# A recommendation tower in one kernel: first-layer weight first in the load queue, id tables over ScalarE's queue, context split and context transposes moved behind the weight tables

## The reference

```python
e = jnp.stack([tbl_0[ids[:, 0]], ..., tbl_25[ids[:, 25]]], axis=1)       # (512, 26, 32)
x1 = einsum('bik,bjk,hij->bhk', e, e, W1) + b1                           # (512, 128, 32)
x2 = einsum('bik,bjk,hij->bhk', x1, e, W2) + b2                          # (512, 128, 32)
z = concatenate([x1, x2], axis=1).sum(axis=-1)                           # (512, 256)
h = concatenate([z, dense_ctx], axis=1)                                  # (512, 272)
h = maximum(h @ W_top1 + b_top1, 0)                                      # 272 -> 512
h = maximum(h @ W_top2 + b_top2, 0)                                      # 512 -> 256
y = h @ W_top3                                                           # (512, 1)
```

## Time and profile before

| | |
|---|---|
| median of 3 runs | 152.55 us (152.45 to 153.67) |
| the profiled execution's own time | 151.98 us |
| its span, first to last instruction | 150.2 us |
| PE busy | 129.0 us (86%) |
| DVE busy | 103.0 us (69%) |
| POOL busy | 87.8 us (58%) |
| ACT busy | 73.9 us (49%) |
| mean granted TensorE clock | 0.966 of full speed |

### The profile page before, as it was taken

How to read it: one execution, slowest core, us unless ns; L and a number is a source line. 1 busy time by engine, 2 the same in 40 slices (tenths; PEclk the granted TensorE clock), 3 DMA queues, 4 the chain that set the end, 5 groups by cost and what they waited for, 6 DMA issues and landing times.

```text
span 150.2 us, 5238 instructions
## 1 busy us (share of the span) xinstructions
PE 129.0 (86%) x2218; PEld 114.3 (76%) x2218; DVE 103.0 (69%) x351; ACT 73.9 (49%) x201; POOL 87.8 (58%) x96
## 2 busy tenths in 40 slices
PE   5335999983988689988999998899999889699994
PEld 5323666753987579988879998887999877599992
DVE  7889583999999999789159969937994993000000
ACT  1220488487767874718658401363930146590042
POOL 3787777777788777777777777777777100000000
PEclk9955599999999999999999999999999999999999
DMA  6976438620013130100103220011332000311000
GB/s 116 387 157 176 117 135 213 194 74 20 13 18 59 40 82 13 18 13 13 18 18 61 72 54 13 14 18 18 60 83 48 5 0 4 52 45 54 0 0 1
DMA packets 9065, 9.36 MB, mean 62 GB/s; under 512 B 3089, under 2 KB 8047, under 8 KB 8862
## 3 DMA queue, kind: packets, MB, share of 16 engines
q1 hardware_dynamic: 5678, 7.55, 17.5%
q0 software_dynamic: 2816, 1.45, 7.1%
q10 hardware_dynamic: 548, 0.04, 0.3%
HBM read 7.99 MB, written 1.04 MB: 60 GB/s over the span
## 4 chain that ended last, share of the span: by engine, by line
PE 60%; DVE 17%; SPq 8%; DMA 7%; ACT 3%; issue 3%; DVEq 0%
PE h2y L746 16%; PE h2y L751 8%; DMA octet<-in_octet_ids 7%; PE ring L702 7%; PE ring L710 5%; DVE l L569 5%; PE h2y L801 5%; SPq L310 3%; SPq L314 3%; PE ring L730 3%; PE ring L680 2%; PE ring L739 2%; PE h1p L792 2%; DVE vh_in L443 2%; PE ring L703 2%
## 5 line engine op out<-in xcount | busy, mean ns | idle before, releaser
L350 POOL DMA_INDIRECT emb<-in_tbl,idx x88 | 86.9, 988 | 28.2 <-issue 26.5
L746 PE MATMUL h2y<-t_in,v_in 128*128 128x128 f32 x208 | 24.3, 276 | 0.0
L746 PEld LDWEIGHTS h2y<-t_in,v_in 128*128 128x128 f32 x208 | 23.7, 192 | 0.2
L667 PE MATMUL ring<-w1s,w2t 128*128 128x352 f32 x52 | 18.3, 515 | 3.5 <-DVE w1s L404 3.5
L912 ACT COPY t_in<-ring 128x416 f32<-128x416 f32 x32 | 15.2, 537 | 11.3 <-PE ring L703 11.3
L702 PEld LDWEIGHTS ring<-r,l 64*64 64x64 f32 x512 | 16.4, 134 | 4.5 <-issue 2.1
L702 PE MATMUL ring<-r,l 64*64 64x52 f32 x512 | 18.1, 220 | 1.6 <-issue 1.2
L667 PEld LDWEIGHTS ring<-w1s,w2t 128*128 128x128 f32 x52 | 11.1, 215 | 9.9 <-DVE w1s L404 3.6
L703 PE MATMUL ring<-r,l 64*64 64x52 f32 x512 | 18.3, 220 | 0.0
L703 PEld LDWEIGHTS ring<-r,l 64*64 64x64 f32 x512 | 16.5, 134 | 0.0
L569 DVE TENSOR_TENSOR l<-sg_b,l 128x192 f32<-128x192 f32 (+5 forms) x72 | 16.1, 299 | 0.2
(11 more groups left out here) (133 smaller groups left out, 209.5 us busy)
## 6 DMA issues: line engine op xcount, KB each, us to landing
w2t<-in_L_rec_W SPq DMA_DIRECT2D x1, 1664.0 KB, 7.0
emb<-in_tbl,idx POOLq DMA_INDIRECT x88, 3.0
wt<-in_W_top SPq DMA_DIRECT2D x2, 512.0 KB, 8.8
small_tbl<-in_tbl SPq DMA_DIRECT2D x8, 125.0 KB
octet<-in_octet_ids SPq DMA_DIRECT2D x1, 750.0 KB
gram_scratch<-t_in SPq DMA_DIRECT2D x4, 169.0 KB
gram<-gram_scratch SPq DMA_DIRECT2D x4, 126.0 KB
w<-in_L_rec_W SPq DMA_DIRECT2D x1, 338.0 KB, 7.3
```

The costliest lines, as they stand in the source:

```text
L350: pool.indirect_dma_start(out=emb[:, g, f * K:(f + 1) * K], out_offset=None, in_=a[f"tbl_{f}"][:, :], in_offset=bass.IndirectOffsetOnAxis( ...
L667: last = pe.matmul(ps[:, 0:PR + MIX], w2t[:, c, :], w1_of[c // NH], start=True, stop=True)
L746: last = pe.matmul(z2p, v_in[:, j, :], t_in[:, j, :], start=(start and j == j0), stop=(stop and j == j1 - 1))
```

## The change

Four things are moved; no instruction of the computation is added or removed.

1. On SP's queue W1 goes ahead of W2.
2. The two parts of `octet` and `place_in` are issued by ACT, behind its small rows, where SP issued them before.
3. DVE does the W1 tables (L384 to L409) right behind its first clears; the context split, the clear of `t_ac` and the clear of half of `R` come behind them. `one_hot_rest` goes ahead of `split_wt1c`.
4. On PE (and ACT) the "small" entry of `pre` is first, and the context transposes stand between mix 8 and mix 9. In the first group's `z_group` the second look-up for group 1 stands behind the first 13 products, where it stood behind the gram products.

```diff
-OH_FIRST, OH_FIRST_AT = 2, 18
+OH_FIRST, OH_FIRST_AT, CTX_AT = 2, 18, 9
...
-        pre = [("ctx", 0, 0), ("small", 0, 0)]
-        pre += [("mix", x, 1) for x in range(NF)]
+        pre = [("small", 0, 0)]
+        pre += [("mix", x, 1) for x in range(CTX_AT)] + [("ctx", 0, 0)] + [("mix", x, 1) for x in range(CTX_AT, NF)]
...
             sp.dma_start(idx[:, :, :], a["ids"].rearrange("(g p) f -> p g f", p=P)).then_inc(ids_in, 16)
+            sp.dma_start(w1[:, :, :], a["L0_rec_W1"]).then_inc(w1_in, 16)
             sp.dma_start(w2t[:, :, :], a["L0_rec_W2"]).then_inc(w2_in, 16)
-            sp.dma_start(w1[:, :, :], a["L0_rec_W1"]).then_inc(w1_in, 16)
-            sp.dma_start(octet[0:OR, 0:OH_FIRST, :, :], a["octet_ids"][:, 0:OH_FIRST, :, :]).then_inc(octet_first, 16)
-            sp.dma_start(place_in[:, :, :], a["place_ids"]).then_inc(place_loaded, 16)
...
-            sp.dma_start(octet[0:OR, OH_FIRST:NP, :, :], a["octet_ids"][:, OH_FIRST:NP, :, :]).then_inc(octet_rest, 16)
...
-            dve.memset(t_ac[P // 4:HALF, :, :], 0.0).then_inc(gap_zeroed, 1)
-            dve.wait_ge(ctx_loaded, 16)
...
-            dve.memset(R[:, 0:NT // 2, :, :], 0.0)
             dve.wait_ge(w1_in, 16)
...
+            dve.wait_ge(ctx_loaded, 16)
+            x = ctx_in
...
+            dve.memset(t_ac[P // 4:HALF, :, :], 0.0).then_inc(gap_zeroed, 1)
+            dve.memset(R[:, 0:NT // 2, :, :], 0.0)
...
             one_hot()
+            one_hot_rest()
             split_wt1c()
-            one_hot_rest()
...
                 if kind == "small":
+                    keep_warm(WARM_CTX, h1p[:, 0, :])
...
                     across(start=True)
+                    look_up(1, 1)
                     for n in range(LATER, len(pre)):
                         prepare(n)
                     pe.wait_ge(pre_out, LATER)
                     inner(0, NH)
                     gram_part(g)
-                    look_up(1, 1)
...
+            act.dma_start(octet[0:OR, 0:OH_FIRST, :, :], a["octet_ids"][:, 0:OH_FIRST, :, :]).then_inc(octet_first, 16)
+            act.dma_start(octet[0:OR, OH_FIRST:NP, :, :], a["octet_ids"][:, OH_FIRST:NP, :, :]).then_inc(octet_rest, 16)
+            act.dma_start(place_in[:, :, :], a["place_ids"]).then_inc(place_loaded, 16)
```

More of the change, by code:

```diff
@@ L409, in _ @@
             dve.tensor_copy(w1g[:, NH * NF:GR].rearrange("p (u v) -> p u v", v=NH), w1[:, NH:NF, NH:NF]).then_inc(w1_ready, 1)
+            dve.wait_ge(ctx_loaded, 16)
+            x = ctx_in
+            for n, part in enumerate(("hi", "mid", "lo")):
+                dve.tensor_copy(ctx_part[:, :, :], x[:, :, :]).then_inc(ctx_split, 1)
+                dve.wait_ge(ctx_split, 2 * n + 2)
+                for s in range(SLOTS):
+                    if CTX_SLOTS[s] == part:
+                        last = dve.tensor_copy(ctx_x[:, :, s, :], ctx_part[:, :, :])
+                if n < 2:
+                    last = dve.tensor_tensor(ctx_rest[n][:, :, :], x[:, :, :], ctx_part[:, :, :], ALU.subtract)
+                    x = ctx_rest[n]
+                last.then_inc(ctx_split, 1)
+                dve.wait_ge(ctx_split, 2 * n + 3)
+            dve.memset(t_ac[P // 4:HALF, :, :], 0.0).then_inc(gap_zeroed, 1)
+            dve.memset(R[:, 0:NT // 2, :, :], 0.0)
             def mixed(c, x0, x1, quarters):
@@ L655, in prepare @@
                 elif kind == "ctx":
-                    keep_warm(WARM_CTX, h1p[:, 0, :])
                     pe.wait_ge(ctx_split, 7)
```

## The result

The changed kernel takes 155.97 us (155.16 to 156.43), the kernel before 152.69 in the same rounds. The ratio is 1.0188, with a 95% interval of 1.0146 to 1.023: **slower by 1.9%**, and outside the range of the prediction, 150.9 to 154.4. The profiled execution took 155.99 us; its span is 154.2, 4.0 more than before, while the medians differ by 3.3. An execution falls at times into a second state, some per cent slower: the ratios are of executions outside it, and of the traces shown only e4's (154.55 us) lies in it.

The account below looks back on a forecast made before the run. PE looked like the bound, with DVE bounding the front and a gather chain 0.25 us behind at the end. The front end's 3.5 us shrink to 0.1: span 150.1, median 152.45 us, range 150.9 to 154.4.

Parts of the forecast that it names:

- `octet` over ACT: Front-end loads: issued near 4 us in place of 14.07, the rest of `octet` lands by 15; DVE reaches it at 16 to 17.
- If these land at 19.19 as before: DVE's order: with context rows landing then, first embeddings could start at 22.66 in place of 26.90, 4.2 us earlier.
- the sum: Whole kernel: the front end's 3.5 us shrink to 0.1 at the end, because PE waits for DVE at groups 2 and 3.
- the second chain: Ids, 86 gathers, 7.12 us of DVE, `t_block` of group 3: independent of the change, ends 0.25 us ahead of the first.
- E: Slower: `octet` shares DMA engines with W2 and context rows; W2 after 13 or context rows after 23; 153 to 155; chance 0.05.
- W1's tables: Start of DVE's front end: W1 lands and tables can start at about 4.7 us, where DVE started them at 10.00.
- First mix: PE's front end: starts at 10 us in place of 13.11, 3.1 us off the start (0.1 to 4.0).
- The context transposes within the mixes: PE's row of mixes: they cost at most about 1.1 us there, and are not on the end's path.
- rival A: End of kernel: gathers set the end; gain 0.1 us, time 152.45, 151.2 to 153.7; chance 0.66.
- rival B: Faster: gathers lose less than their 3.75 us; saving 2 gives 150.4, all about 149; chance 0.14 for savings over 1.4.
- The wait of 2.6 us: `t_block` of group 2: PE would arrive at 94.45 and wait for DVE's fill, until 97.04.
- D: Slower: clock falls in PE's new wait at `t_block` of group 2; 2.5 us of work lost, 154.3, up to 156; chance 0.12.

Follow-up runs that it names:

- e4: e8 with the eight context loads ahead of the small tables on SP's queue; 153.08 us, ratio 1.001.
- e5: Changed kernel with each load of `octet` and the small tables (125 partitions) cut into 112 and 13 partitions; 151.56 us, ratio 0.9887.
- e6: Kernel before with the loads of `octet` and the small tables cut into 112 and 13 partitions; 150.98 us, ratio 0.9859.
- e2: Kernel before with only the two `octet` loads and `place_in` issued by ACT behind its small rows; 157.06 us, ratio 1.0288.
- e3: Changed kernel with 30 more warming matmuls on PE ahead of the look-up for group 1; 155.05 us, ratio 1.0154.
- e1: Changed kernel with the `octet` loads and `place_in` back on SP's queue and `one_hot_rest` back behind `split_wt1c`; 152.68 us, ratio 1.0006.
- e7: e5 with four of group 0's gathers replaced by plain loads of the tables' first rows, so its embeddings are wrong; 148.51 us, ratio 0.9691.
- e9: Changed kernel with only the `octet` loads cut into 112 and 13 partitions, small tables uncut; 151.94 us, ratio 0.9923.
- e8: Changed kernel with `place_in` ahead of the two `octet` loads on ACT's queue; 154.81 us, ratio 1.0104.

## Why the prediction was wrong

**The step that failed** is the one on "`octet` over ACT": "Even with the 10.88 us that it took it has landed by 15, and DVE comes to it at 16 to 17", and with it the "if" of the next step, "If these land at 19.19 as before". The rest of `octet` had landed at about 21.3 and DVE came to it at 23.54; the context rows landed at 26.26. The 10.88 us were what the load took from its issue late in SP's order. Issued at 3.5, it had W2 (packets to 9.13) and the first part of `octet` (7.16 to 12.59) ahead of it, and it shared few engines with the first four tables of 125 KB: its own packets ran from 12.29 to 21.28. From 7.16 to that end the 1000 KB of `octet` went at 71 KB/us, where W1 and W2 (128 partitions) went at 255 before. From 10 to 15 us the DMA share was 0.42, by which (an estimate) 6.7 of 16 engines were at work on average for all loads together; with the cut it was 1.09. No gain from the second queue shows: e5, which has it among its changes, is no faster than e6, which hasn't.

The Trainium skill (DMA: Bandwidth & Descriptors, Why a DMA increments its semaphore by 16 and not by 1) says that a transfer goes to the largest number of engines, up to 16, that divides its slowest dimension; worked out from that, 5 for 125 partitions, 16 for 112, 13 for 13. By that rule the cut must spread the load; the traces agree (busy share 0.42 to 1.09, and 5 packets of `octet` at once in the changed kernel against 16 in e5), while which of the engines were used no run here shows. The Trainium skill (DMA: Bandwidth & Descriptors, Issuing engines are not separate DMA queues) says that another issuing engine saves only the time of the issue; e2, at 1.0288, agrees in that nothing else was saved.

Three things followed, none of them in the sum. `place_in` stands behind `octet` on ACT's queue, and lands after 18.3 us: **a moved load takes those behind it along**, and I had priced two of the three issues. SP's own issues were held up, one of them for 6.72 us; that its tables found their engines taken is how I read it, and in e5, where the loads are spread, the same eight context loads take SP 4.22 us, in e4, where they stand ahead of the tables, 4.02. And so the context rows landed at 26.26 in place of 19.19. DVE's front came at 29.66, where 22 to 24 was forecast: 6.7 us worse at the middle, of which the second chain hid what it would have hidden of the gain. What shows at the end is the later part alone. Of the 4.0 us between the profiled executions, 2.76 are the later first embeddings (29.66 for 26.90) and 0.5 to 0.9 the clock (e3); some 0.3 to 0.7 no run settles.

**The rival that came true** is E, "the loads collide", at a chance of 0.05. Its threshold was right ("context rows after 23") and its size nearly (153 to 155), but the two rows that spoke for it were read for the wrong question. The earlier trace rows show 750 KB in 10.88 us, 69 KB/us, beside the 255 KB/us of W1 and W2 that the same text works with; the earlier trace rows show a DMA share of 0.53 from 13 to 18 us, while tables, context rows and `octet` were still outstanding. Here a load that was slow while the engines were half idle was bound by its own shape, and next to another of the same shape it got slower still. Of E's two ways only one came: W2 landed at 10.3, not after 13. And the time, 155.97, is above its 155.

**Right, by its steps.** W1's tables: forecast for 4.7, came at 4.80; but the share of 338 in 2002 KB that the text names doesn't give 4.7, so the hit is in part luck. First mix: "I take 10", a choice between 9.1 and 13, came at 10.42; W2 landed 8.5 us after its issue. The context transposes within the mixes cost no time that shows (e1, 1.0006). The look-up moved brings nothing that shows. The second chain exists and caps the gain of a better front: in e5 and e6 `t_block` of group 3 begins 0.10 us behind DVE's fill, and e7 takes the wait away. With the front end as forecast, e5's 151.56 lies in rival A's range (151.2 to 153.7) and e6's 150.98 just below it. But the gain isn't A's 0.1. It comes mostly from the gathers, a piece of rival B: gather 86 starts at 112.89 in e5 and 112.32 in e6, where it started at 113.35 before, and in e6 the fill ends 1.37 us earlier (121.83 for 123.20) of the 1.52 by which `t_block` of group 3 does. In the changed kernel too gather 86 starts earlier, at 112.31. Why the gathers lost less isn't shown; the long gather of the earlier trace rows lies on two passes over `octet`, and no trace tells in what mode these run. So the second chain isn't "independent of everything that the change moves". The wait of 2.6 us that the sum has at group 2 is in no trace.

**Half right.** D's mechanism, a fall of the clock in a long wait of PE, came, but in the wait ahead of the look-up (7.91 us) and not at `t_block` of group 2, and cost 0.5 to 0.9 us at the end, not 2.5. In e1 the same fall, in a wait of 6.07, cost nothing that shows. By D's own terms 10 us at half speed would give 156.8, where it has 156.

## What to carry to other kernels

Before a load is moved to another queue "to run in parallel", divide its bytes by its landing time and look at the DMA share of that stretch: in this kernel the slow loads had too few engines, and cutting their partitions (125 into 112 and 13) paid where moving them didn't. Count what is queued behind the moved load, small ones above all, and what the queue that it left will be held up by. And read the slack of the next-late chain first: here it was 0.25 us, so the front end could lose without limit, and could gain little beyond what the gathers gave.

## What the hardware showed that I had not expected

- 1000 KB ahead of it on the second queue took a load of 8 KB from 9.6 to 18.3 us to its landing, and SP was held for 6.72 us in one issue (before, 4.67 at most); with the loads cut in two, 269 GB/s moved from 10 to 15 us in place of 115.
- Of a load of 125 partitions 5 packets were under way at once (6 or 7 for moments in some traces), of one of 128 some 16 to 19.
- The clock was down after the waits of 3.09 us (e7), 4.86 (e9), 5.56 (e4), 6.07 (e1), 6.38 (e2), 7.56 (e8) and 7.91 (the change) ahead of the look-up, and not after those of 0.48 (e6), 2.14 (e5) and 2.86. The length of the wait isn't all: ahead of the mixes PE waited 3.69 us in the change and 3.62 in e5, and from 10 to 15 us the clock was at 1.00 in the one and at 0.50 in the other. A fall cost 0.5 to 0.9 us in one kernel (e3) and nothing that shows in another (e1).
- Four gathers fewer gave 3.05 us by the medians, where 2.15 are explained by the start of `t_block`; PE's stops without a releaser, 2.69 us in e5 and 1.73 in e7, end 1.2 to 1.5 us after a fetch of 16 KB of instructions.
